# Gated cross-attention and feed-forward on one core: Q, K and V projected already turned, operands of the scores stacked by way of device memory

## The chip, the cores and the metric

The kernel runs on one core of a Trainium2 chip. The metric is the device time of one execution, in microseconds (us). The engines are TensorE (PE in the profile; its weight loads are PEld), VectorE (DVE), ScalarE (ACT), GpSimd (POOL) and SyncE (SP), which here only issues DMAs. A small q behind an engine's name, as in SPq, means its sequencer.

## What is computed

Eight batches of 128 tokens, 512 features each, go through a gated cross-attention and a gated feed-forward. There are 32 query heads of 16 features and 8 key/value heads, each shared by 4 query heads. All inputs are float32.

```python
x = x + tanh(g_xattn[0]) * xattn(layernorm(x), ctx, ctx, Wq, bq, Wk, bk, Wv, bv, Wo, bo)
x = x + tanh(g_ffn[0]) * ffn(layernorm(x), w1, w1_scale, w3, w3_scale, w2, w2_scale)

# xattn
Q = query @ Wq + bq; K = key @ Wk + bk; V = value @ Wv + bv    # heads: 8 x 4, 8, 8, of 16 features
scores = einsum('bhgqd,bhkd->bhgqk', Q, K) / sqrt(16)
w = softmax(scores, axis=-1)
y = einsum('bhgqk,bhkd->bhgqd', w, V)                          # back to 512 features
return y @ Wo + bo
# ffn, 512 -> 1792 -> 512, weights scaled by block of 128 x 128
h = silu(x @ w1.T) * (x @ w3.T); return h @ w2.T
```

## The kernel before

**Precision.** Every float32 operand of a matmul is split into a high part in TensorE's faster float32r form and the rest: names in H and L (`WpH` and `WpL`, `xTH` and `xTL`). A product is three matmuls, high by high, high by low, low by high; `three` at line 1765 issues them, which is why lines 1767 to 1769 carry most of TensorE's work. ACT makes most high parts and DVE or POOL most low ones.

**Attention, batch by batch.** POOL splits a tile of the context (`ct`) into `ctH` and `ctL`. DVE and POOL make the statistics of the layer norm, ACT writes the normalised `xn`, TensorE turns it (`turn4`) and ACT and DVE split the result into `xTH` and `xTL`. `project_kv` makes K and V (12 matmuls of 256 columns a batch) and `project` makes Q (12 of 512 columns); a further matmul each adds the bias (`add_bias`). In these the tokens are the stationary operand, so Q, K and V come out with tokens on the partitions. For the scores they are wanted with features on the partitions, and the three products of a score are folded into one matmul of 96 rows: 32 rows of high, 32 of low and 32 of high queries against high, high and low keys. So ACT and DVE write `Qtok` and `Ktok` with these copies side by side, TensorE turns them (`stack_q`, `stack_k`, through `identr`, line 1774; 24 turns a batch), and ACT copies the turned ones to `Qst` and to the stacked keys (`kst`, in the upper part of `x2HL`, which is not yet needed for its own purpose). V is cut into three bf16 parts in `Vp`.

**Scores.** `scores(n, h)` computes scores with queries on the partitions, only for their maximum along the keys (`row_max`, DVE, line 1142). The maxima are split in two (`Mtok`), turned to rows (`turn_max`), copied (`Mrow`) and moved by four small DMAs (`max_in`) into rows 96 to 99 of `Qst`, one pair of heads each; matching rows of the keys select the head. `scores_t(n, g)`, line 1819, computes the scores again with keys on the partitions and the maximum already subtracted. ACT takes its exponential twice, as float32 (`E`) and as f16 (`PH`), and POOL makes `PL`, the difference of the two (line 340, 64 of them). `values` multiplies with `Vp`; DVE sums the three parts and divides. The result is turned, projected with Wo in four blocks, added to `X`, normalised, turned and split into `x2H` and `x2L` (`x2HL`).

**Feed-forward.** 14 chunks of the 1792 features for two halves of four batches: `gu` computes both branches of a chunk, `y` the product back, 36 matmuls of 512 columns a chunk. POOL scales the weights (`scale`, line 351), ACT and DVE split them.

**Order.** All orders are written out by hand per engine: each engine's block issues its operations in one fixed sequence with semaphore waits between them. Queue SP loads in that order too, and a wait on SP holds back everything behind it. TensorE's list mixes projections of later batches, scores, values and the first chunks of the feed-forward. `W0`, `W1` and `W2` are three PSUM banks for whatever is turned or projected; two more hold the scores and two their transposed form, one the values.

## Time and profile before

| | us |
|---|---|
| median of 3 runs | 392.64 (391.22 to 392.65) |
| the profiled execution | 391.85 |
| its span, first to last instruction | 390.1 |
| TensorE busy | 377.4 |
| VectorE busy | 271.7 |
| ScalarE busy | 209.1 |
| GpSimd busy | 160.5 |

The profile is of one execution. Its span leaves out what lies around the program, 1.75 us here. Busy times are the time in which at least one instruction of an engine runs; matmuls overlap, so that two of 0.40 us may start 0.23 apart, and the sum of the durations is more than the busy time. An engine's idle time costs something only if another one waits for what it does later.

### The profile page before, as it was taken

The numbers are of one execution on the slowest core, as the hardware profiler recorded it, in microseconds if no ns is written. First come the engines' busy times: TensorE is split into PE (matmuls) and PEld (weight loads), VectorE is DVE, ScalarE is ACT, GpSimd is POOL, SyncE is SP. The second block draws the span as 40 slices with busy tenths as digits, with TensorE's granted clock in tenths as the row PEclk, the third lists the DMA queues.
The fourth block names the chain that finished last, engine by engine and source line by source line (L and its number), as shares of the span: only waits on it lengthen the run. The fifth ranks groups of instructions, "written<-read, shape, count | busy, mean of one in ns | idle before, by whom it ended". The sixth has DMA issues, their size and how long they took to land.

```text
span 390.1 us, 6293 instructions
## 1 busy us (share of the span) xinstructions
PE 377.4 (97%) x2350; PEld 307.5 (79%) x2350; DVE 271.7 (70%) x452; ACT 209.1 (54%) x367; POOL 160.5 (41%) x135
## 2 busy tenths in 40 slices
PE   7789999999998999999999999999999999999996
PEld 5578888888887677878888888888888888888885
DVE  5978998979998967898776777543954344554334
ACT  4678999998999986552332332332332332332320
POOL 6558889898999785264333443000000000000000
PEclk9999999999999999999999999999999999999999
DMA  8903104100000040295000000000200000000002
GB/s 289 342 14 86 32 2 167 46 40 6 2 6 3 3 166 2 86 416 227 0 0 0 0 0 0 0 0 2 108 0 0 0 0 0 0 0 0 0 0 108
DMA packets 6817, 20.98 MB, mean 54 GB/s; under 512 B 875, under 2 KB 1131, under 8 KB 6668
## 3 DMA queue, kind: packets, MB, share of 16 engines
q1 hardware_dynamic: 6364, 19.92, 14.0%
q10 hardware_dynamic: 432, 0.79, 0.5%
q8 instruction: 13, 0.21, 0.2%
q14 instruction: 8, 0.07, 0.0%
HBM read 18.28 MB, written 2.10 MB: 52 GB/s over the span
## 4 chain that ended last, share of the span: by engine, by line
PE 83%; DVE 9%; DMA 3%; SPq 2%; ACT 1%; issue 1%; POOL 0%; DVEq 0%
PE ps L1767 23%; PE ps L1769 23%; PE ps L1768 22%; PE ps L1819 3%; PE ps L1809 3%; PE ps L1774 3%; DMA gsc<-in_small 3%; DVE MX L1142 2%; PE ps L1827 2%; PE ps L1775 1%; PE ps L1828 1%; DVE x2HL L1172 1%; DVE X L1183 1%; DVE aTL L1153 1%; DMA Qst<-Mrow 1%
## 5 line engine op out<-in xcount | busy, mean ns | idle before, releaser
L1767 PE MATMUL ps<-x2HL,w13H 128*128 128x512 f32 x224 | 89.1, 398 | 0.0
L1769 PE MATMUL ps<-x2HL,w13L 128*128 128x512 f32 x224 | 88.6, 395 | 0.0
L1768 PE MATMUL ps<-x2HL,w13H 128*128 128x512 f32 x224 | 88.4, 395 | 0.0
L340 POOL TENSOR_TENSOR PL<-E,PH 128x512 f16<-128x512 f32 x64 | 74.1, 1174 | 13.2 <-ACT E L609 7.2
L351 POOL TENSOR_TENSOR wres<-wres,gsc 128x1536 f32<-128x1536 f32 x14 | 42.5, 3037 | 44.2 <-DVE hf L1196 44.2
L632 ACT ACTIVATE T<-ps 128x512 f32<-128x512 f32 x28 | 16.7, 597 | 79.0 <-PE ps L1769 79.0
L640 ACT ACTIVATE hH<-hf 128x512 fp32r<-128x512 f32 x28 | 17.7, 632 | 63.5 <-DVE hf L1196 63.5
L1769 PEld LDWEIGHTS ps<-x2HL,w13L 128*128 128x128 f32 x224 | 42.0, 187 | 10.4
L1768 PEld LDWEIGHTS ps<-x2HL,w13H 128*128 128x128 f32 x224 | 42.0, 188 | 9.8
L1189 DVE SCALAR_TENSOR_TENSOR A<-T,ps 128x512 f32<-128x512 f32 x28 | 19.2, 685 | 43.8 <-ACT T L632 43.8
L1767 PEld LDWEIGHTS ps<-x2HL,w13H 128*128 128x128 f32 x224 | 42.0, 188 | 9.5
L1767 PE MATMUL ps<-w2H,hH 128*128 128x512 f32 x112 | 44.3, 396 | 0.6 <-DVE x2HL L1172 0.6
L1205 DVE TENSOR_TENSOR hL<-hf,hH 128x512 fp32r<-128x512 f32 x28 | 43.2, 1541 | 2.5
L1769 PE MATMUL ps<-w2H,hL 128*128 128x512 f32 x112 | 43.8, 391 | 0.0
L1768 PE MATMUL ps<-w2L,hH 128*128 128x512 f32 x112 | 43.5, 389 | 0.0
L1142 DVE TENSOR_REDUCE MX<-ps 128x8 f32<-128x1024 f32 x32 | 38.9, 1215 | 4.6 <-PE ps L1809 4.6
L1196 DVE SCALAR_TENSOR_TENSOR hf<-A,ps 128x512 f32<-128x512 f32 x28 | 19.2, 687 | 32.5 <-PE ps L1769 32.2
L609 ACT ACTIVATE E<-ps 128x512 f32<-128x512 f32 x64 | 38.2, 612 | 1.8 <-PE ps L1819 1.6
L1177 DVE TENSOR_TENSOR w13L<-wres,w13H 128x1024 fp32r<-128x1024 f32 x28 | 34.1, 1219 | 5.1 <-ACT w13H L627 5.1
L612 ACT ACTIVATE PH<-ps 128x512 f16<-128x512 f32 x64 | 37.1, 606 | 1.0 <-PE ps L1819 0.6
L627 ACT ACTIVATE w13H<-wres 128x1024 fp32r (+1 forms) x28 | 29.3, 1045 | 0.0
L1819 PE MATMUL ps<-Qst,x2HL 100*128 100x512 f32 x64 | 27.3, 439 | 0.1
(112 smaller groups left out, 712.8 us busy)
## 6 DMA issues: line engine op xcount, KB each, us to landing
wres<-in_wff SPq DMA_DIRECT2D x14, 768.0 KB, 6.7
X<-in_x SPq DMA_DIRECT2D x8, 256.0 KB, 11.1
ct<-in_ctxt SPq DMA_DIRECT2D x7, 256.0 KB, 3.2
raw<-in_wproj SPq DMA_DIRECT2D x3, 512.0 KB, 6.3
out<-X SPq DMA_DIRECT2D x6, 256.0 KB, 2.0
raw<-in_wproj SPq DMA_DIRECT2D x1, 1024.0 KB, 9.4
Qst<-Mrow SPq DMA_DIRECT2D x32, 8.0 KB
out<-X ACTq DMA_DIRECT2D x2, 256.0 KB, 2.1
```

Of the source, the lines that this page charges most:

```text
L340: pool.tensor_tensor(PL[:, g % NL, :], E[:, g % NE, :], PH[:, g, :], ALU.subtract).then_inc(pL_ok, 1)
L351: pool.tensor_tensor(w, w, v, ALU.mult).then_inc(scaled, 1)
L609: act.activation(E[:, g % NE, :], ps[:, g % 2, :], ACT.Exp, scale=SCALE).then_inc(E_ok, 1)
L612: act.activation(PH[:, g, :], ps[:, g % 2, :], ACT.Exp, scale=SCALE).then_inc(PH_ok, 1)
L627: act.activation(w13H[:, s, :], wres[:, n, 0:W13], ACT.Copy).then_inc(w13H_ok, 1)
L1142: dve.tensor_reduce(MX[:, :, h, :], ps[:, 2:4, :].rearrange("p b (j g k) -> p (b j) g k", j=2, g=2), AX.X, ALU.max).then_inc(max_ok, 1)
L1177: dve.tensor_tensor(w13L[:, s, :], wres[:, n, 0:W13], r32(w13H[:, s, :]), ALU.subtract).then_inc(w13L_ok, 1)
L1205: dve.tensor_tensor(hL[:, s, :], hf[:, s, :], r32(hH[:, s, :]), ALU.subtract).then_inc(hL_ok, 1)
L1767: pe.matmul(out_ap, aH, bH, start=start, stop=False)
L1768: pe.matmul(out_ap, aH, bL, start=False, stop=False)
L1769: return pe.matmul(out_ap, aL, bH, start=False, stop=stop)
L1819: pe.matmul(ps[:, g % 2, :], kst(n)[0:ROWS + 4, g % 2, g // 2, :], Qst[0:ROWS + 4, n % 2, g // 2, :], start=True, stop=True).then_inc(st_p ...
```

## The change

Q, K and V are projected the other way round: the weights are the stationary operand and the tokens, of two batches at once, the moving one (256 columns). The features of Q, K and V then stand on the partitions without a turn, and the biases, now one number per partition, are added by ACT and DVE in the operation that copies the result out of PSUM (`q_high`, `k_high`, `v_bias`). V is turned back by two plain turns for each pair of batches (`turn_v`). To bring 32 rows of a pair of heads and the copies high, low, high above one another, the high and low parts go out to two tensors in device memory, `qscr` and `kscr`, and come back by one read of 32 rows for each of the three places (`queries_in`, `keys_in`; for the first batch by halves, `queries_part`).

The rows that carry the maxima are 16 and not 4, so `scores_t` contracts 112 rows and not 100, and one DMA brings them (`max_in`, 9 DMAs and not 32; the first batch has two). Scores are grouped by the query head in the group and not by the pair. Statistics have two slots each; some small operations went from DVE to POOL (`epsilon`, `shift`, `max_low`), and high parts of the context from POOL to ACT. The written orders of all five engines are new. Loads come in another order, and TensorE starts with 16 and not 14 warm-up matmuls.

```diff
+        qscr = nc.dram_tensor("qscr", [NBATCH // 2, 2, 2, P, GJ * P], F32).ap()
+        kscr = nc.dram_tensor("kscr", [NBATCH // 2, 2, P, 2, TWO], F32).ap()
...
+        def keys_out(eng, p, low):
+            eng.dma_start(kscr[p, low], r32((KTL if low else KTH)[:])).then_inc((kh_out, kl_out)[low], 16)
+
+        def keys_in(eng, p, t):
+            s = (NBATCH - NKST + 2 * p % NKST) * P
+            eng.dma_start(r32(kall(32 * t, 32 * t + 32)[:, :, s:s + TWO]),
+                         kscr[p, t % 2].rearrange("(r h) g n -> r (h g) n", h=PAIRS)).then_inc((k_in0, k_in1)[p % 2], 16)
...
+        def queries_in(eng, n, t, done):
+            eng.dma_start(r32(Qst[32 * t:32 * t + 32, n % 2, :, :]).rearrange("r h n -> r (h n)"),
+                         qscr[n // 2, t // 2, n % 2].rearrange("(r h) n -> r (h n)", h=PAIRS)).then_inc(done, 16)
...
+            sp.wait_ge(kT_H, 2)
+            keys_out(sp, 0, 0)
+            sp.wait_ge(kh_out, 16)
+            keys_in(sp, 0, 0)
+            sp.wait_ge(qT_H, 2)
+            queries_out(sp, 0, 0, 0, 2, qh_outa)
...
             sp.wait_ge(mrows, 5)
...
+            max_in(sp, 3, 0, 4)
+            sp.wait_ge(qh_out, 48)
+            sp.wait_ge(st_ps, 24)
+            queries_in(sp, 4, 0, q_in0)
+            queries_in(sp, 4, 1, q_in0)
...
+            def q_high(bank, j):
+                act.wait_ge(bias_in, 16)
+                act.activation(QTH[:, :, j, :], bank[:, 0:TWO].rearrange("p (b q) -> p b q", b=2), ACT.Identity,
+                               bias=biasT[:, BQ + j:BQ + j + 1]).then_inc(qT_H, 1)
...
+            def project_q(bank, j, k0, k1):
+                for k in range(k0, k1):
+                    c = Q0 + (j // 2) * KB * TWO + k * TWO + (j % 2) * P
+                    w = slice(c, c + P)
+                    m = three(bank[:, 0:TWO], WpH[:, w], WpL[:, w], xTH[:, k, :, :], xTL[:, k, :, :], k == 0, k == KB - 1)
+                return m
```

**Where instructions stand now.** TensorE at the start, before: the end of batch 0's Q projection, and all up to the first `scores` (line 1809).

```order
L1793 MATMUL ps<-brow,ones 128x512
L1774 MATMUL ps<-identr,Ktok 96x128 x4
L1775 MATMUL ps<-ident,xn 128x128 x4
L1774 MATMUL ps<-identr,Qtok 96x128 x8
L1774 MATMUL ps<-identr,Ktok 96x128 x4
L1774 MATMUL ps<-identr,Qtok 96x128 x4
L1809 MATMUL ps<-x2HL,Qst 128x256 x4
```

The same place after: the last rows before the first `scores` (line 1937), which are K and V of batches 2 and 3 and the turn of `xn` of batch 3.

```order
L1895 MATMUL ps<-ctH,WpH 128x256
L1896 MATMUL ps<-ctL,WpH 128x256
L1897 MATMUL ps<-ctH,WpL 128x256
L1903 MATMUL ps<-ident,xn 128x128 x4
L1937 MATMUL ps<-x2HL,Qst 128x256 x8
L1895 MATMUL ps<-xTH,WpH 128x256
```

The 20 turns through `identr` ahead of the first scores are gone; 96 matmuls of 256 columns stand there now, where there were 13 of 256 and 13 of 512.

SP after, at the start: from the first wait of its list on. `L209` loads Wo, `L206` tiles of X, `L212` `boT`; `L218` writes keys out and `L222` reads them, `L226` writes queries out and `L234` reads them.

```order
L245 DMA ct<-in_ctxt 128x512 [waits ctL_ok_dve]
L209 DMA raw<-in_wproj 128x2048
L206 DMA X<-in_x 128x512 x2
L212 DMA boT<-in_small 128x512
L218 DMA kscr<-KTH 128x512 [waits kT_H]
L222 DMA x2HL<-kscr 32x8x256 [waits kh_out]
L226 DMA qscr<-QTH 128x2x256 [waits qT_H]
L226 DMA qscr<-QTL 128x2x256 [waits qT_L]
L203 DMA x2HL<-sel 16x8x128
L222 DMA x2HL<-kscr 32x8x256 [waits kl_out]
L226 DMA qscr<-QTH 128x2x256 [waits qT_H,qT_H_dve]
L226 DMA qscr<-QTL 128x2x256 [waits qT_L]
```

Before, SP had nothing but loads there, the selection rows and, at its first wait for `mrows`, the rows of maxima.

SP after, in the middle: from the maxima of batch 3 to those of batch 4.

```order
L238 DMA Qst<-Mrow 16x4x512 [waits mrows]
L230 DMA Qst<-qscr 32x2048 [waits st_ps,qh_out]
L230 DMA Qst<-qscr 32x2048
L218 DMA kscr<-KTL 128x512
L230 DMA Qst<-qscr 32x2048 [waits st_ps]
L230 DMA Qst<-qscr 32x2048
L238 DMA Qst<-Mrow 16x4x512 [waits mrows]
```

Before, four DMAs of 4 rows stood behind each wait for `mrows` and nothing of the queries; now reads of the queries wait for the last `scores_t` of the batch whose place they take, with a third read of each batch in ACT's list.

## Rows read from the trace of the kernel before

**Rows 1.** Stretches: length, busy of PE, PEld, DVE, ACT, POOL; clock, DMA share, GB/s.

```profile
0.00:19.10 19.10, 13.77 (x68) 10.47 (x68) 14.04 (x28) 10.54 (x16) 11.14 (x25) 1.00 0.90 320
19.10:33.00 13.90, 12.62 (x102) 11.08 (x101) 10.46 (x20) 10.08 (x17) 8.72 (x6) 1.00 0.12 31
33.00:149.40 116.40, 114.25 (x1134) 95.26 (x1132) 103.18 (x235) 109.59 (x217) 102.50 (x90) 1.00 0.13 45
149.40:169.10 19.70, 19.33 (x120) 15.20 (x118) 16.16 (x33) 10.38 (x18) 8.26 (x7) 1.00 0.30 112
169.10:390.00 220.90, 217.48 (x936) 175.48 (x936) 127.87 (x139) 68.50 (x103) 29.86 (x10) 1.00 0.08 32
```

**Rows 2.** The longest wait of TensorE but the first: us in total, times, longest.

```profile
PE ps L1774 <- DVE Mtok L1149: 1.6, 3, 0.8
```

**Rows 3.** TensorE's groups by shape: count, then busy us and mean ns of one.

```profile
L1774 PE MATMUL ps<-identr,Qtok 128*96 128x128 f32 x128 | 13.7, 233 | 1.6 <-DVE Qtok L1127 1.2 <-ACT x2HL L615 0.3
...
L1774 PE MATMUL ps<-identr,Ktok 128*96 128x128 f32 x64 | 6.9, 231 | 0.3 <-DVE Ktok L1107 0.3
L1863 PE MATMUL ps<-Ktok 128*128 128x512 f32 x14 | 5.6, 578 | 1.8 <-DVE Ktok L1073 1.8
L1775 PE MATMUL ps<-ident,xn 128*128 128x128 f32 x32 | 5.0, 277 | 0.3 <-DVE vres L1118 0.2
```

**Rows 4.** TensorE's timeline from 20.31 us: start, duration, instruction.

```profile
20.31 0.28 PE L1769 MATMUL ps<-WpH,ctL 128*128 128x256 f32 x1
20.43 0.40 PE L1767 MATMUL ps<-WpH,xTH 128*128 128x512 f32 x1
20.66 0.39 PE L1768 MATMUL ps<-WpL,xTH 128*128 128x512 f32 x1
...
21.12 0.42 PE L1774 MATMUL ps<-identr,Qtok 128*96 128x128 f32 x4
21.37 0.70 PE L1809 MATMUL ps<-x2HL,Qst 96*128 96x256 f32 x4
```

**Rows 5.** ACT's groups by shape: the copies of turned queries and keys.

```profile
L619 ACT ACTIVATE Qst<-ps 96x512 fp32r<-96x512 f32 x32 | 18.7, 598 | 0.9 <-PE ps L1774 0.7
...
L615 ACT ACTIVATE x2HL<-ps 96x512 fp32r<-96x512 f32 x16 | 9.8, 612 | 2.0 <-PE ps L1774 2.0
```

**Rows 6.** DVE's groups by shape: the row maxima and their low parts.

```profile
L1142 DVE TENSOR_REDUCE MX<-ps 128x8 f32<-128x1024 f32 x32 | 38.9, 1215 | 4.6 <-PE ps L1809 4.6
...
L1149 DVE SCALAR_TENSOR_TENSOR Mtok<-MX,Mtok 128x32 fp32r<-128x32 f32 x8 | 2.4, 300 | 0.0
```

**Rows 7.** POOL's groups by shape between 33 and 152 us.

```profile
L340 POOL TENSOR_TENSOR PL<-E,PH 128x512 f16<-128x512 f32 x64 | 74.1, 1174 | 13.2 <-ACT E L609 7.2 <-ACT PH L612 5.4 <-PE ps L1828 0.2
L337 POOL TENSOR_TENSOR X<-X,boT 128x512 f32<-128x512 f32 x7 | 9.1, 1306 | 0.0
L351 POOL TENSOR_TENSOR wres<-wres,gsc 128x1536 f32<-128x1536 f32 x3 | 8.3, 2762 | 0.0
L334 POOL TENSOR_TENSOR ctL<-ct,ctH 128x512 fp32r<-128x512 f32 x5 | 6.4, 1288 | 0.0
L331 POOL TENSOR_TENSOR ctH<-ct,unit 128x512 fp32r<-128x512 f32 x4 | 4.2, 1038 | 0.6 <-DMA ct<-in_ctxt 0.6
L324 POOL TENSOR_TENSOR rs<-ve,neghalf 128x1 f32<-128x1 f32 x4 | 2.3, 566 | 0.7 <-DVE ve L1097 0.7
```

**Rows 8.** Timeline of the first 20 us: first statistics, first scores.

```profile
3.97 0.69 DVE L1091 BATCH_NORM_STATS2 st<-X 128x6 f32<-128x512 f32 x1
...
19.17 0.71 PE L1809 MATMUL ps<-x2HL,Qst 96*128 96x256 f32 x4
```

**Rows 9.** DMA: a store's issue to landing, maxima on the chain, a loading stretch.

```profile
out<-X SPq DMA_DIRECT2D x6, 256.0 KB, 2.0
...
58.82 2.29 DMA Qst<-Mrow
...
8.00:10.00 2.00, 1.04 (x7) 0.77 (x6) 1.32 (x2) 1.68 (x3) 0.00 (x0) 1.00 0.97 367
```

More of the change, by code:

```diff
@@ L1275, in _ @@
+            max_high(0, 2)
             dve.wait_ge(s_ps, 4)
[L1276 removed]
+            row_max(0, 3)
+            mean(5)
             dve.wait_ge(max_ok, 4)
[L1278 to L1289 removed]
@@ L1801, in stack_q, with project_kv @@
[L1801 to L1810 removed]
+            def project_kv(bank, w0, k0, k1):
+                for k in range(k0, k1):
+                    w = slice(w0 + k * KVD, w0 + (k + 1) * KVD)
+                    m = three(bank[:, 0:TWO], WpH[:, w], WpL[:, w], ctH[:, k, :, :], ctL[:, k, :, :], k == 0, k == KB - 1)
+                return m
```

2723 lines of the change are left out of this document (1338 added, 1385 removed).

## The prediction

> **What bounds the kernel now.** I read the stretches first: each engine's busy time in five pieces of the span, cut at the first `scores` (19.1 us), the first and the last `scores_t` (33.1 and 149.4) and the first matmul of `y` (169.1) [rows 1]. In the feed-forward stretch TensorE is busy 217.5 of 220.9 us and the others far less: only TensorE counts there. In the 116.4 us between the `scores_t` TensorE has 114.3, but ACT 109.6, DVE 103.2 and POOL 102.5: four engines with little room, and whatever relieves one meets the next. The waits of TensorE [rows 2] show how little is idle: the longest, apart from the one before the warm-up, is 1.6 us for DVE's `Mtok`, in three pieces. Only the first 33 us are another matter; there TensorE is busy 26.4 us, 5.6 of them warm-up matmuls [rows 3].
>
> TensorE's busy times overlap, so I price its work by the distance from one start to the next [rows 4]: a matmul of 256 columns takes 0.12 us (20.31 to 20.43), one of 512 takes 0.23 (20.43 to 20.66), four turns through `identr` 0.25 (21.12 to 21.37), so 0.063 each. The granted clock is 1.00, the 2.4 GHz level, in every stretch [rows 1].
>
> **The change, TensorE's work.** Gone are 128 turns of `Qtok` and 64 of `Ktok` [rows 3], 192 x 0.063 = 12.1 us, and 16 bias matmuls, eight of each width, 8 x 0.23 + 8 x 0.12 = 2.8. The Q projection goes from 96 matmuls of 512 columns to 192 of 256: 96 x 0.23 = 22.1 becomes 192 x 0.12 = 23.0, 0.9 more. K and V stay at 96 of 256. Eight plain turns of V come in, at no more than the 5.0 / 32 = 0.16 us of the turns of `xn` [rows 3]: 0.9 to 1.3. That is 14.9 - 0.9 - 1.1, some 13 us less; with the two new warm-up matmuls under the loads at nothing.
>
> **ACT, DVE, POOL.** ACT loses 32 copies to `Qst` at 0.60 and 16 to the stacked keys at 0.61 [rows 5], 29 us, and gets back some 25 half-width copies, at about 0.4: it drops out of the argument. DVE keeps its 32 reductions of 1.2 us [rows 6]; small operations on V and `Mtok` give way to half-width ones out of PSUM. I take 8 us less between the `scores_t`: 95. POOL keeps its 64 `PL` at 1.17 us, and loses less than TensorE does. Counted from its first `PL` to its last [rows 7]: 64 x 1.17 = 75.1; three `scale` at 2.76, 8.3; three bias additions instead of seven, 3.9; two `ctL` instead of four, 2.6; one `ctH`, 1.0; seven roots at 0.57, 4.0; seven `max_low` and eleven single-column operations that are new on POOL. No row has these on POOL. The nearest above is a root, 0.57, and below they cost at least nothing; I take 0.25, nearer to DVE's 0.30 for the same `Mtok` operation [rows 6], 4.5 in all. Sum 99.4 us (94.9 to 105.2), where before the same sum was 107.
>
> **The stretch between the `scores_t`, 116.3 us now.** By TensorE's order it loses 75 matmuls of 512 columns (177 to 102), gains 79 of 256 (169 to 248), and loses 144 small turns and 4 plain ones: -17.3 + 9.5 - 9.1 - 0.5 = -17.4, hence 98.9. That is more than a proportional share of the 13 us, since the projections of the first four batches' K and V now stand ahead of the first scores. But POOL wants 99.4 by then. Two engines cannot both be at 100% of a stretch while handing work to each other through four buffers of `E` and `PL`; before, the leader had 98% and the second 94%. I put POOL at 96%: 99.4 / 0.96 = **103 us**, a gain of 13 and not 17. The cover that hid POOL's sum was TensorE's own length, and it is gone.
>
> **The start, 33.1 us now.** Here the detour through device memory is bare. The high half of the keys is ready at about 14 us: X lands before 3.97 [rows 8], the first weights soon after, then come two normalisations, two turns and the projection. But its write stands in SP's ring behind what SP has asked for by 10 us: six tiles of X, three of `ct`, `boT`, Wv (11 x 0.25 MB), Wq and Wo (1 MB each), 4.75 MB, with 1.3 MB on ACT's ring drawing from the same engines. 6.1 MB (6.4 million bytes) at the 320 GB/s of the first 19 us [rows 1] is 20 us; the write itself 0.8 and the landing 1.5 more (a store lands 2.0 after its issue, issue 0.45 included [rows 9]): 22.3. SP waits there (`kh_out`), and so do all its later DMAs and, behind the same semaphore, ACT's `q_high(W2, 3)`, `normalise(2)` and its own reads. From 22.3 SP issues six DMAs at 0.55 and one selection read at 0.8 before the read of the queries, 26.4; it lands 2.3 us later, as a row of maxima does [rows 9], and a little more for its size: first `scores` at **29.3**, where now it is 19.17 [rows 8]. TensorE has done 13 us of projections by then and is idle some 8 us.
>
> Then DVE sets the pace: `row_max(0, 0)` is queued behind `x_low(3, W2)`, whose turn came just before the scores, to about 30.5. Four reductions at 1.2 make 35.4, split and subtraction 0.6 and 0.3 [rows 6] with waits 1.0, turn and copy 0.8, issue and landing 2.9 as for a row of maxima: first `scores_t` at **40**, 7 us later than now. From the first `scores` it has 11 us, as against 13.9 now, of which TensorE's own work is 9.
>
> **Edits with one answer.** In the feed-forward nothing but the place of two buffers changes: 220.9 stays. From the last `scores_t` to `y` there are 66 matmuls of 512 columns where 69 were, with four more plain turns: 19.7 becomes 19.4. The larger selection matrix costs POOL some 3 us before 7 us, under the loads. The maxima now go in one DMA of 16 rows and not in four of 4 rows at 0.58 us each of SP: no one waits longer.
>
> **The sum.** 40 + 103 + 19.4 + 220.9 = 383.3 us of span, where it is 390.1. The profiled execution took 391.85, 1.75 over its span; 385.1. The median of the runs is 0.8 above the profiled one, the lowest 0.6 below; I give 385.5.
>
> **Where a page speaks against it.** Six times, a stage's queries are read anew as soon as the last `scores_t` of the batch two before has let go of the `Qst` slot, and `scores` of the new batch stands 3.5 to 4.7 us of TensorE work behind it. Three reads of 256 KB each: issues to 1.1, landing 1.5, bytes 0.79 MB at the 367 GB/s of [rows 9] 2.1, so 4.7 after the slot is free; with waits elsewhere the stretch of TensorE is 4 to 5 long, a stall near nothing. That rate is one of tiles of 128 partitions; no row has a large read into 32. The Trainium skill, page "SBUF — State Buffer", section "Door 1: The DMA port swizzle", holds that partitions 0 to 31 reach only 8 of 16 ports, and measures 189 GB/s against 328 at 1 MiB. By that the three reads would move their bytes in 4.2 us and the stall would be about 2 us each time; the trace before can't tell, and I carry it as a rival.
>
> **The rivals.**
> A, the engines interlock better than I think: TensorE keeps the lead, the stretch is 98 us and the start 38 (the queue drains at the 367 GB/s of [rows 9], 2.5 us sooner). 38 + 98 + 19.4 + 220.9 + 2.2 = 378.5. For it: TensorE is busy 98% of the stretch with ACT at 94% and POOL at 88% beside it [rows 1]. Against: POOL's sum alone is 99.
> B, slower than before: reads into 32 rows move at half of 367 GB/s. Then each of six batches waits 6.8 - 4.4 = 2.4 us (14 us), and the first scores wait 1.5 more. 385.5 + 14 less what POOL catches up in those waits (its sum is then no bound, 4 us) = 395.5 to 397. It decides from about 1 us of stall a batch, where the gain is below measuring.
> C, the start is longer and nothing else: SP's blocking waits stack up (a read that lands 3 us late delays three more), TensorE comes back at the lower clock, where the warm-up matmuls took 0.40 each and not 0.23 [rows 3]. First `scores_t` at 45: 390.5, no change.
> D, the change doesn't do what it says, since the turns were hidden anyway: excluded for TensorE, busy 98% of the stretch [rows 1]; if POOL's unknown operations cost 0.57 each, the stretch is 105.2 / 0.96 = 109.6 and the time 392.
>
> **How the numbers follow.** Forecast 385.5 (382 to 389): 0.42. A: 0.26. B: 0.15. C: 0.10. D: 0.07. A measurement here tells some 0.5% from no change, 2 us: faster means under 390.7, slower over 394.6. Faster has the forecast, A and a little of C and D: 0.70. Slower has B and a tail: 0.16. Same 0.14. The range from 376 to 396 reaches from under A to the nearer part of B and leaves out some 2 in 10.
>
> **What would show it.** In the changed profile: no turns of `Qtok` and `Ktok`; the first `scores` near 29 us after an idle TensorE and the first `scores_t` near 40; the stretch between the `scores_t` at 103 with POOL busiest of all and waits of TensorE for `PL` and its releasers; the feed-forward unchanged at 221. Waits of the first `scores` matmul of a batch for a DMA of `Qst` above 1 us would mean B. The prediction is wrong if the first `scores` come before 25, or if the stretch is under 99 us or over 108.

## The result and the profile after

The changed kernel takes 417.11 us (median of 4 runs, 413.38 to 418.77), the kernel before 391.94 (4 runs, 391.22 to 392.65): ratio 1.063, 95% interval 1.054 to 1.072. The forecast was 385.5 us, the range ended at 396. The profiled execution took 418.76 us, one of the two longest of the four, so what is read from this one profile carries a spread of some 5 us.

The same five stretches as in [rows 1], cut at the same four matmuls (first `scores`, first and last `scores_t`, first matmul of `y`): length, busy of PE, PEld, DVE, ACT, POOL; granted clock, DMA share, GB/s.

```profile
span 417.0 us, 6079 instructions
0.00:32.20 32.20, 22.56 (x130) 19.90 (x130) 21.44 (x45) 17.31 (x28) 16.23 (x21) 0.93 0.87 283
32.20:46.60 14.40, 12.08 (x79) 11.90 (x80) 9.92 (x18) 4.24 (x9) 9.37 (x12) 0.79 0.89 212
46.60:174.00 127.40, 112.05 (x988) 92.46 (x986) 96.25 (x199) 87.08 (x168) 94.60 (x96) 0.87 0.48 127
174.00:194.40 20.40, 18.92 (x120) 14.98 (x119) 16.27 (x27) 7.16 (x13) 10.19 (x14) 1.00 0.41 159
194.40:417.00 222.60, 217.71 (x938) 175.32 (x936) 129.46 (x140) 69.99 (x104) 31.01 (x10) 1.00 0.07 27
```

| stretch, us | before | forecast | after |
|---|---|---|---|
| to the first `scores` | 19.1 | 29.3 | 32.2 |
| to the first `scores_t` | 13.9 | 10.7 | 14.4 |
| between the `scores_t` | 116.4 | 103 | 127.4 |
| to the first `y` | 19.7 | 19.4 | 20.4 |
| to the end | 220.9 | 220.9 | 222.6 |

Of the 33.7 us by which the span misses the forecast, 24.4 are in the middle, 6.6 at the start, 2.7 behind. And the clock is no longer at 2.4 GHz throughout: 0.93, 0.79 and 0.87 granted in the first three stretches, where [rows 1] had 1.00 everywhere. The page by 40 slices says where:

```profile
PE   6867979897897889997999999999999999999996
PEclk9896998896999759999999999999999999999999
DMA  8989682981544304019500000000020000000002
DMA packets 16949, 37.60 MB, mean 90 GB/s; under 512 B 1984, under 2 KB 7616, under 8 KB 16128
```

The clock dips again and again up to slice 15 of 40, that is through nearly all attention batches, and so does TensorE's busy share; the DMA engines move 37.6 MB (21.0 before), most of it by 160 us. What TensorE waits for in the whole span, beside [rows 2], where the longest wait was 1.6 us:

```profile
PE ps L1937 <- DMA Qst<-qscr: 15.6, 8, 2.5
PE ps L1903 <- DVE xTL L1221: 3.3, 1, 3.3
PE ps L1903 <- ACT xn L741: 2.2, 1, 2.2
PE ps L1895 <- DVE xTL L1221: 1.8, 2, 1.5
```

L1937 is `scores`: eight waits for the queries from device memory, six of them between the `scores_t`, one a batch from the third on. One of these in TensorE's timeline (start, duration, instruction, idle before):

```profile
110.02 0.18 PE L1957 MATMUL ps<-Vp,PL 128*128 128x49 bf16 x1
112.05 0.74 PE L1937 MATMUL ps<-x2HL,Qst 96*128 96x256 f32 x4 [1.85 <-DMA Qst<-qscr]
...
113.30 0.62 PE L1896 MATMUL ps<-WpL,aTH 128*128 128x512 f32 x1
113.72 0.63 PE L1897 MATMUL ps<-WpH,aTL 128*128 128x512 f32 x1
114.14 0.63 PE L1895 MATMUL ps<-WpH,aTH 128*128 128x512 f32 x1
114.57 0.63 PE L1896 MATMUL ps<-WpL,aTH 128*128 128x512 f32 x1
...
116.95 0.40 PE L1897 MATMUL ps<-WpH,aTL 128*128 128x512 f32 x1
```

TensorE is idle 1.85 us, and 1 us later its matmuls of 512 columns stand 0.43 us apart and last 0.63, where [rows 4] has 0.23 and 0.40: the 1.2 GHz level, for some 3.5 us. The wait is paid, and then the clock.

The issues of these reads (KB each, median us from issue to landing), at this wait and, below, between 31.3 and 42.4 us, where batch 1's are under way with much else:

```profile
Qst<-qscr SPq DMA_DIRECT2D x2, 256.0 KB, 4.7
Qst<-qscr ACTq DMA_DIRECT2D x1, 256.0 KB, 4.7
...
Qst<-qscr SPq DMA_DIRECT2D x2, 256.0 KB, 7.0
```

The first reads of a batch are asked for the moment its slot is free; from the first issue (106.36 us here) to the last landing (112.01) it is 5.65 us, over the six batches 5.6 to 6.9. The forecast had 4.7. The work that TensorE does between that first issue and its wait is 3.7 to 5.0 us in the six batches (3.8 here, to 110.20), about as forecast (3.5 to 4.7).

### The profile page after: what moved, and what is told of

Read it like the earlier page. It is cut to its first block, busy times and chain, and to the rows that moved or that the text cites. A ratio compares the mean times of both kernels' runs of the same rounds, so it can differ in the third digit from the quotient of the medians.

```text
span 417.0 us, 6079 instructions
## 1 busy us (share of the span) xinstructions
PE 383.3 (92%) x2248; PEld 314.6 (75%) x2248; DVE 273.3 (66%) x426; ACT 185.8 (45%) x318; POOL 161.4 (39%) x151
## 4 chain that ended last, share of the span: by engine, by line
PE 74%; DMA 14%; ACT 4%; DVE 4%; SPq 3%; issue 1%; ACTq 0%; DVEq 0%
PE ps L1895 21%; PE ps L1897 21%; PE ps L1896 20%; DMA Qst<-qscr 10%; PE ps L1937 4%; PE ps L1948 3%; PE ps L1903 2%; DMA ct<-in_ctxt 2%; ACT E L772 2%; ACT PH L775 1%; DMA kscr<-KTH 1%; DMA qscr<-QTH 1%; PE ps L1956 1%; PE ps L1957 1%; DVE MX L1261 1%
## 5 line engine op out<-in xcount | busy, mean ns | idle before, releaser
L455 POOL TENSOR_TENSOR PL<-E,PH 128x512 f16<-128x512 f32 x64 | 75.2, 1191 | 22.6 <-ACT E L772 9.4
L775 ACT ACTIVATE PH<-ps 128x512 f16<-128x512 f32 x64 | 38.3, 606 | 18.6 <-PE ps L1948 18.5
L1937 PE MATMUL ps<-x2HL,Qst 96*128 96x256 f32 x128 | 27.5, 351 | 17.4 <-DMA Qst<-qscr 15.6
L1937 PEld LDWEIGHTS ps<-x2HL,Qst 96*128 96x128 f32 x128 | 24.1, 249 | 21.9 <-issue 11.3
L1318 DVE TENSOR_TENSOR w13L<-wres,w13H 128x1024 fp32r<-128x1024 f32 x28 | 35.0, 1249 | 5.4 <-ACT w13H L790 5.4
```

What stands on the lines that cost most here:

```text
L455: pool.tensor_tensor(PL[:, g % NL, :], E[:, g % NE, :], PH[:, g, :], ALU.subtract).then_inc(pL_ok, 1)
L775: act.activation(PH[:, g, :], ps[:, g % 2, :], ACT.Exp, scale=SCALE).then_inc(PH_ok, 1)
L1318: dve.tensor_tensor(w13L[:, s, :], wres[:, n, 0:W13], r32(w13H[:, s, :]), ALU.subtract).then_inc(w13L_ok, 1)
L1937: m = pe.matmul(ps[:, b + h // 2, (h % 2) * TWO:(h % 2 + 1) * TWO], Qst[0:ROWS, n % 2, h, j * P:(j + 1) * P], kst(n)[0:ROWS, 2 * h:2 * h + ...
```

## The experiments

Sixteen more kernels ran, each beside the kernel before on the same chip (391.3 to 391.4 us). The time is the median of all executions of a kernel. "First `scores_t`" and "stretch" are of one profiled execution; the stretch is the one between the first and last `scores_t`. How far such a stretch can be trusted is seen on the kernels whose middle is that of the changed kernel, but for the split of Wo in some: e8, e3, e7, e14, the changed kernel itself and e10 have 122.7, 123.1, 124.5, 127.2, 127.4 and 127.9 us. A difference of under 5 us between two stretches shows nothing by itself. The profiles of e4, e8 and e16 are of their shortest executions (405.3, 417.2 and 400.9 us), that of e10 is of its longest (420.5).

| | time, us | ratio to before (95%) | first `scores_t` | stretch |
|---|---|---|---|---|
| after | 417.11 | 1.063 (1.054 to 1.072) | 46.6 | 127.4 |
| e1 reads left out | 398.32 | 1.017 (1.014 to 1.021) | 47.6 | 104.8 |
| e2 idle matmuls | 410.36 | 1.049 (1.045 to 1.053) | 46.8 | 118.6 |
| e3 reads in the quiet stretch | 414.68, once | | 46.8 | 123.1 |
| e4 reads into 96 rows | 407.27 | 1.039 (1.035 to 1.044) | 47.8 | 112.6 |
| e6 three places | 413.54 | 1.054 (1.046 to 1.062) | 45.5 | 116.2 |
| e7 turn first | 414.61 | 1.058 (1.055 to 1.061) | 46.6 | 124.5 |
| e8 Wo later | 422.40 | 1.083 (1.079 to 1.087) | 49.7 | 122.7 |
| e9 e6, e7 and e8 | 416.01 | 1.065 (1.060 to 1.070) | 49.0 | 115.8 |
| e10 start | 417.81 | 1.063 (1.057 to 1.069) | 47.7 | 127.9 |
| e11 maxima by ACT | 412.15 | 1.052 (1.049 to 1.055) | 48.0 | 119.3 |
| e12 e10 and e11 | 413.03 | 1.054 (1.051 to 1.058) | 46.8 | 120.8 |
| e13 maxima first | 407.85 | 1.042 (1.039 to 1.046) | 46.6 | 116.3 |
| e14 late loads | 418.37 | 1.064 (1.057 to 1.071) | 45.9 | 127.2 |
| e15 e13 and idle matmuls | 404.04 | 1.033 (1.028 to 1.039) | 46.0 | 113.5 |
| e16 e15, 64 rows | 403.89 | 1.032 (1.030 to 1.034) | 45.4 | 110.6 |
| e17 e16, reads first | 403.94 | 1.031 (1.028 to 1.035) | 44.9 | 113.6 |

### What the reads cost: e1

```diff
-            queries_in(sp, 2, 1, q_in0)
-            queries_in(sp, 2, 0, q_in0)
...
-            pe.wait_ge(q_in0, 96)
             scores(2, 0)
```

> Part left out: the reads of the stacked queries of batches 2 to 7 (18 reads of 256 KB) and TensorE's waits for them; the scores of these batches are made from what stands in the slot, everything else is as in the changed kernel. If the waits for these reads, with what the clock does after them, are the loss (theory R), the stretch between the first and the last scores_t falls from 127.4 us to 103 to 108 and the time from 417 to 393 to 398. If the new orders of the engines or POOL's sum are the loss (theory O), the stretch stays above 120 us and the time above 410. The start (first scores_t at 46.6) should not move under either.

398.32 us, and the stretch (same columns as above):

```profile
47.60:152.40 104.80, 98.92 (x987) 81.10 (x986) 95.37 (x199) 85.69 (x168) 94.28 (x95) 1.00 0.38 109
```

Theory R holds and O falls: by these two profiles 22.6 of the 24.4 us lost in the middle are the reads of the queries and what follows from waiting for them (18.3 if e3's 123.1 is taken for the changed kernel's stretch), and 1.8 are left for the new orders of the engines. The time falls by 18.8 us. The clock is 1.00 in this stretch. It also shows that reads at no cost would not have saved the change: 398.3 is 1.7% slower than before (1.4 to 2.1%), by the start, since the first `scores_t` is still at 47.6 us and not at 33.1.

### What the clock costs: e2

```diff
+                for _ in range(m):
+                    pe.matmul(bank, WpH[:, 0:P], WpH[:, 0:DM], start=True, stop=True)
...
+            fill(ps[:, 2, :], 9)
             pe.wait_ge(q_in0, 96)
             scores(2, 0)
```

> The changed kernel with nine matmuls of 512 columns on constant operands ahead of each of the six waits for the queries of batches 2 to 7, written to the bank that the scores overwrite next; 9 x 0.22 = 2.0 us, as long as the waits of 2.0 to 2.6 us. They do nothing useful, TensorE is only not idle. If a good part of the loss is the lower granted clock after each wait (theory C), scores start no later than now, the matmuls behind them go at 0.12 us a 256 columns and not 0.21, the granted clock of the stretch goes from 0.87 to 0.95 or more, and the stretch from 127.4 to about 116: time 404 to 408. If the clock costs nothing here, the time stays at 417, or grows by up to 3 us where the nine matmuls outlast the wait.

```profile
46.80:165.40 118.60, 112.22 (x1041) 91.97 (x1040) 95.10 (x199) 86.36 (x168) 94.64 (x96) 0.99 0.53 136
```

From TensorE's last useful matmul to the `scores` it is 12.2 us in the six places together, as long as before, but now filled with work that does nothing. The stretch is 8.8 us shorter by the two profiles (4.5 against e3's, which has the same waits, 12.0 us, and a clock of 0.90), the time 6.8 us, and the granted clock goes from 0.87 to 0.99. That is less than expected (404 to 408): theory C holds, its size was too high. With e1 the 22.6 us come apart: 12.2 are the six waits for `Qst<-qscr` in this stretch, 8.8 the clock behind them, 1.6 are left. The 1.6 may well be one wait that e2 has and the changed kernel has not, before a `scores_t`:

```profile
PE ps L1952 <- DMA Qst<-Mrow: 1.7, 1, 1.7
```

### Rows, bytes, latency: e3 and e4

e3 is the changed kernel with a series of reads in the quiet feed-forward stretch:

```diff
+                probe([(flat[0:32, :], src[0:32, :])])
+                probe([(E[:, 0, :], qscr[0, 0, 0])])
+                probe([(flat[32 * t:32 * t + 32, :], src[32 * t:32 * t + 32, :]) for t in range(3)])
+                probe([(E[:, t, :], qscr[0, t // 2, t % 2]) for t in range(3)])
+                probe([(flat[0:96, :], src[0:96, :])])
+                probe([(flat[0:64, :], src[0:64, :])])
+                probe([(flat[0:16, 0:512], src[0:16, 0:512])])
```

> The changed kernel with reads from device memory into a tile that is no longer used, issued by SP in the quiet feed-forward stretch, one after the landing of the one before, the series twice: one read of 256 KB into 32 rows, one of 256 KB into 128 rows, three into 32 rows each (rows 0, 32, 64), three into 128 rows each, one of 96 rows x 8 KB, one of 64 rows x 8 KB, one of 16 rows x 2 KB. If the few rows set the rate (theory P), one read into 32 rows takes over 0.6 us longer than one into 128, and three of them about 2 us longer than three into 128 rows, 5.5 against 3.7. If it is the way there and back (theory L), all series differ by their bytes at one rate, and even the small read takes over 2.5 us.

The DMA issues of the first series in the order of the list, one line for each entry (KB each, median us to landing):

```profile
E<-qscr SPq DMA_DIRECT2D x1, 256.0 KB, 3.3
...
E<-qscr SPq DMA_DIRECT2D x1, 256.0 KB, 2.7
...
E<-qscr SPq DMA_DIRECT2D x3, 256.0 KB, 4.2
...
E<-qscr SPq DMA_DIRECT2D x3, 256.0 KB, 3.1
...
E<-qscr SPq DMA_DIRECT2D x1, 768.0 KB, 5.3
...
E<-qscr SPq DMA_DIRECT2D x1, 512.0 KB, 4.7
...
E<-qscr SPq DMA_DIRECT2D x1, 32.0 KB, 1.7
```

From the first issue to the last landing, three reads into 32 rows took 5.5 us (5.4 in the second series), three into 128 rows 4.1 (4.5). The smallest took 1.7 (1.8). So both theories have a part, though theory L had put the small read above 2.5 us: some 1.7 us go by before even 32 KB have landed, and the bytes of three reads on top take 3.8 us into 32 rows and 2.4 to 2.7 into 128, 0.9 to 1.4 us less and not the 2 expected by P. 64 rows in one read (512 KB, 4.7 us) go no faster than two reads of 32 (the second landed 4.5 us after the first was asked for), and 96 rows in one (5.3, then 5.0) little faster than three times 32. The Trainium skill, page "SBUF — State Buffer", section "Door 1: The DMA port swizzle", holds that rows 0 to 63 reach no more ports than rows 0 to 31; the traces here agree with that, and with 32 rows being slower than 128, by a factor of 0.63 to 0.75 in the bytes' part (the page's 189 against 328 GB/s is 0.58).

e4 changes the shape in place:

```diff
+                c = slice(684 * t, min(684 * t + 684, PAIRS * GJ * P))
+                eng.dma_start(r32(Qst[0:ROWS, n % 2, :, :]).rearrange("r h n -> r (h n)")[:, c],
+                              qscr[n // 2].rearrange("l b (r h) n -> (l b r) (h n)", h=PAIRS)[0:ROWS, c]).then_inc(done, 16)
```

> Part changed: for batches 2 to 7 each of the three reads brings the same 256 KB into all 96 rows, a third of the columns each (96 rows x 2.7 KB and not 32 rows x 8 KB), from other places of the scratch, so the queries are not the right ones; numbers, bytes, queues and the waits for the slot are the same. Theory P (32 rows take the bytes at half the rate): the reads last 4.2 us or less and not 5.6 to 6.9, the waits of scores fall from 2.0 to 2.6 us to under 0.8, the stretch to 110 to 114, the time to 400 to 404. Theory L (latency and total bytes set the length): the waits stay above 1.6 us and the time above 412.

```profile
47.80:160.40 112.60, 101.13 (x987) 82.09 (x986) 95.24 (x199) 86.37 (x168) 94.43 (x95) 0.98 0.51 143
```

Its waits for the queries in this stretch:

```profile
PE ps L1948 <- DMA Qst<-qscr: 7.1, 6, 1.5
```

The time, 407.3, is between the two theories. (The queries that come in are not the right ones; their amount and the waits are.) The reads took 4.8 to 6.4 us, 0.1 to 1.3 less than in the changed kernel, and the six waits 7.1 us in all and not 12.2; the longest is 1.5. With waits 5.1 us shorter the stretch is 14.8 us shorter (the time 9.8), and behind the shorter waits the clock stayed up: 0.98 granted. The 5.1 and the 8.8 that e2 gives to the clock come to 13.9. That is the shape of this loss: over e1's stretch, 12.2 us of waits near 2 us each cost 22.6, and 7.1 us of waits near 1.2 each cost 7.8.

### Asking earlier: e6, e11, e13

```diff
+        def qst(n):
+            if n % 3 < 2:
+                return Qst[:, n % 3, :, :]
+            return Q3[:, :, :]
...
+            sp.wait_ge(qh_out, 32)
+            sp.wait_ge(ql_out, 32)
+            sp.wait_ge(woL_ok, 1)
+            queries_in(sp, 2, 0, q_in0)
+            queries_in(sp, 2, 1, q_in0)
+            queries_in(sp, 2, 2, q_in0)
             sp.wait_ge(mrows, 3)
             max_in(sp, 1, 0, 4)
```

> The changed kernel with three places for the stacked queries and not two: the third lies where the float32 Wo was, so the read of a batch can be asked for when scores_t of the batch three before is done, up to 18 us ahead of its scores; all three reads of a batch of 2 to 7 go on SP, still 32 rows each, the same bytes. The third chunk of feed-forward weights is loaded and scaled later for it. If the loss is that the read cannot start before the slot is free, whatever its rate (theory S), TensorE waits for none of batches 2 to 7, the stretch between the scores_t is 104 to 108 us as without reads, the time 397 to 401. If the bytes of the reads themselves are too many for the time they have, or disturb other work (theory P), waits above 1 us remain at three or more batches and the time is over 406.

413.54 us, above the 406 of theory P, but not for its reason: between the `scores_t` TensorE waits for no queries. What is there in their place (waits in this stretch and, last, one behind it):

```profile
PE ps L1958 <- issue: 3.0, 1, 3.0
...
PE ps L1958 <- DMA Qst<-Mrow: 1.9, 2, 1.7
PE ps L1958 <- DMA Q<-Mrow: 1.5, 1, 1.5
...
PE ps L1913 <- ACT x2n L763: 3.8, 1, 3.8
```

L1958 is `scores_t`, which needs the rows of maxima; the 3.0 us put down to "issue" stand before the first `scores_t` of batch 1, whose maxima landed then. I had put the reads ahead of the maxima on SP. The 3.8 us are another slip of the edit: POOL's moved `scale(2)` holds ACT, and so `x2n`. e11 lets ACT ask for the maxima and moves that `scale`:

```diff
-            sp.wait_ge(mrows, 3)
-            max_in(sp, 1, 0, 4)
...
             max_rows(W0, 0, 4)
+            act.wait_ge(mrows, 3)
+            max_in(act, 1, 0, 4)
```

> The kernel with three places for the queries, and two edits on what it showed: the rows of maxima of batches 1 to 7 are asked for by ACT, behind its own copy, and not by SP, where they stood in the ring behind the reads of the next batch's queries (TensorE waited 1.6 to 3.1 us for them three times); and the third feed-forward chunk is scaled by POOL a batch earlier, since its old new place cost one wait of 4.0 us. Theory Q (what took the place of the wait for queries is the ring in front of the maxima): the waits for Mrow fall under 0.7 us, the stretch from 116.2 to 106 to 109, the time from 413.5 to 400 to 403. If the transfers as such are too many at that time, the waits stay over 1.5 us in any order and the time is above 408.

412.15 us: the maxima were later still. Their DMA on ACT's queue for batch 2, issued at 73.0 us, and below it the same one in the changed kernel on SP's, issued at 73.9 (us to landing):

```profile
Q<-Mrow ACTq DMA_DIRECT2D x1, 128.0 KB, 8.6
```

```profile
Qst<-Mrow SPq DMA_DIRECT2D x1, 128.0 KB, 3.6
```

Nothing stood ahead of it in ACT's queue. But SP asked for 2.5 MB between 71.8 and 75.8 us (queries out, keys in, a weight chunk), 1.5 MB of it before this DMA, since no wait for the maxima held it back any more. The two queues share the DMA engines; the Trainium skill, page "DMA: Bandwidth & Descriptors", says so under "Issuing engines are not separate DMA queues", and the trace agrees, 8.6 us against 3.6. In the changed kernel SP's wait for `mrows` is what keeps the bulk behind the maxima: the same transfers are asked for there from 74.6 us on. e13 makes use of that: three places, SP, and the maxima ahead of the reads.

```diff
-            queries_in(sp, 2, 0, q_in0)
-            queries_in(sp, 2, 1, q_in0)
-            queries_in(sp, 2, 2, q_in0)
             sp.wait_ge(mrows, 3)
             max_in(sp, 1, 0, 4)
+            queries_in(sp, 2, 0, q_in0)
+            queries_in(sp, 2, 1, q_in0)
+            queries_in(sp, 2, 2, q_in0)
```

> Three places for the queries, with the maxima of batches 1, 3 and 5 asked for by SP ahead of the reads of the next batch and ahead of the waits for the scratch, and the third feed-forward chunk scaled a batch earlier. Theory T (the DMA engines serve what was asked for first, on whichever ring: the maxima asked for by ACT landed 8.6 us later behind 2.5 MB that SP had asked for, and 3.1 us later with nothing ahead): all maxima land in under 4.5 us, TensorE waits for neither queries nor maxima more than 1 us between the scores_t, the stretch is 105 to 109 us, the time 398 to 402. If the waits for the maxima had another cause, they stay at 1.5 to 4 us and the time is above 408.

407.85 us, under e11 by 4.3. All maxima now land within 4.1 us of their issue, as theory T expects, but T's time (398 to 402) is missed: the waits went back to the queries (stretch between the `scores_t`):

```profile
PE ps L1947 <- DMA Qst<-qscr: 5.1, 2, 3.4
...
PE ps L1947 <- DMA Q<-qscr: 1.0, 1, 1.0
```

They are before batches 2, 4 and 6, the first of each pair, whose queries must first be written to device memory. So of 127.4 - 104.8 = 22.6 us a third place brings back 11; the other half I did not get by order. The order of the transfers moved waits more than it removed them: e6 has the same stretch, 116.2 us, with 6.4 us of waits for maxima where e13 has 6.1 for queries. The 5.7 us between the times of e6 and e13 lie behind the stretch, where e6 had the slip with `x2n` (26.1 us to the first `y`, 20.6 in e13).

### The start: e7, e8, e9, e10, e12, e14

```diff
-            pe.wait_ge(q_in1, 48)
-            scores(1, 0)
             pe.wait_ge(mL_ok, 2)
             pe.wait_ge(qT_L, 5)
             turn_max(W0, 2, 4)
+            pe.wait_ge(q_in1, 48)
+            scores(1, 0)
```

> The changed kernel, one piece of TensorE's list in another order: the turn of batch 0's last two maxima ahead of scores(1, 0), which waits for batch 1's queries (landed at 42.2 us), and not behind it. If that wait is what holds the first scores_t (it blocks the turn, 2.4 us in the profile), the first scores_t comes at 43 to 44.5 us and not at 46.6, and the time falls by 2 to 3 us to 414 or 415. If DVE's maxima set it as forecast (the last of batch 0 ends at 39.7 us), the turn gains nothing and the time stays at 417.

The first `scores_t` stayed at 46.6. The profile of e7 does not show the wait at all: TensorE was at the lower level there, had no pause from 37 to 42 us, and came to `scores(1, 0)` just after its queries had landed (42.2).

```profile
37.00:42.00 5.00, 5.00 (x26) 4.94 (x26) 3.12 (x6) 1.37 (x3) 1.22 (x4) 0.50 0.93 238
...
42.34 0.71 PE L1937 MATMUL ps<-x2HL,Qst 96*128 96x256 f32 x4
...
46.60 0.39 PE L1948 MATMUL ps<-Qst,x2HL 112*128 112x512 f32 x1
```

In the changed kernel these two matmuls are at 42.33 and 46.59. `scores(1, 0)` stands ahead of `scores_t(0, 0)` in both lists, with 4.3 us of matmuls from the one to the other at the full clock; what is moved ahead of the wait cannot shorten that. The time, 414.6, has an interval that overlaps that of the changed kernel.

```diff
-            out_weights_in(sp)
...
             queries_part(sp, 0, 1, 2, 4, q_in0)
+            out_weights_in(sp)
```

> The changed kernel, with the 1 MB load of Wo behind the reads of batch 0's queries on SP and not ahead of the first write of keys; ACT and POOL split Wo some 20 us later. If the write of the keys waits in the ring behind these bytes (issued at 15.7, landed at 21.3 us), it lands by 18.5 us, the first scores come at 29 to 30 and not at 32.3, the first scores_t at 43.5 to 44.5, the time falls by 2 to 3 us. If the lists of ACT and DVE set the start, the keys land earlier but the first scores stay above 31.3 us and the time within 1 us of 417.

The first write of keys, issued at 15.7 and 15.5 us, in the changed kernel and in e8:

```profile
kscr<-KTH SPq DMA_DIRECT2D x1, 256.0 KB, 5.6
```

```profile
kscr<-KTH SPq DMA_DIRECT2D x1, 256.0 KB, 3.2
```

As expected it lands 2.4 us earlier, and so come the first `scores`, at 29.8 us (forecast 29.3). But the first `scores_t` is 3 us later, and the time 5 longer: the 1 MB of Wo now stands ahead of batch 1's queries, which land at 43.4 us and not 42.2, and the second half of batch 0's queries lands late as well (35.5). e9 has this, the turn and the three places in one:

> The three edits together: a third place for the queries, the turn ahead of the waiting scores, Wo behind the queries' reads. By theory S, and if the two edits of the start each give 2 to 3 us, 399 - 5 = 392 to 396 us, that is still no faster than the kernel before at 391.4; TensorE's work is some 12 us less and the start eats 9 of it. If the start's two edits meet the same limit, only one of them counts and the time is 396 to 398.

416.01 us, 2.5 more than e6 alone, whose slip it carries too: the start's loss (first `scores_t` at 49.0) outweighs. e10 puts batch 1's reads ahead of Wo and of three other tiles:

```diff
-            context_in(sp, 5)
-            select_rows(sp, 3)
             queries_in(sp, 1, 0, q_in1)
+            queries_in(sp, 1, 1, q_in1)
+            out_weights_in(sp)
+            select_rows(sp, 3)
```

> The changed kernel with four moves at the start: Wo out of the way of the first write of keys, as before, but behind the reads of batch 1's queries; those reads ahead of three tiles of ct and X in SP's list; and batch 0's turn of maxima ahead of scores(1, 0). Theory W (the reads of batch 1, landed at 42.2 us behind 1.8 MB of other transfers in SP's ring, hold TensorE at scores(1, 0), and with it scores_t(0, 0), which stands behind): they land by 37 us, the first scores_t comes at 42 to 43.5 and the time is 412 to 414. If ACT's and DVE's lists set the start, the first scores_t stays above 45.5 us and the time above 415.5.

These queries landed at 37.4 us and not 42.2, and the first `scores_t` was still at 47.7; the second half of batch 0's queries came later instead (36.3), and TensorE ran at the lower level:

```profile
30.00:37.00 7.00, 3.73 (x17) 3.47 (x18) 2.68 (x3) 0.30 (x1) 3.04 (x3) 0.50 1.02 271
37.00:42.00 5.00, 5.00 (x26) 4.94 (x26) 3.12 (x6) 0.99 (x2) 0.97 (x4) 0.50 0.87 267
```

This profile is of e10's longest execution (420.5 us), but the other three took 414.2 to 418.8, none in the 412 to 414 of theory W, and e12, which has the same start, shows the same in a usual one: queries landed at 36.8 us, granted clock 0.52 from 30 to 37 us and 0.65 from 37 to 42, first `scores_t` at 46.8. Theory W falls in this form. e12 adds e11 to it, and they don't add up:

> The edits of the start and those of the middle in one kernel. If they add up, first scores_t at 42 to 43.5, stretch 106 to 109, time 396 to 400: still slower than the kernel before (391.4) by what the start costs. If the start's gain is lost in the middle (SP's list is one), the time is 400 to 403 as without it.

413.03 us, against 412.15 for e11 alone. e14 leaves less to be moved before the first `scores_t`, with Wo and a tile of `ct` behind batch 0's maxima.

```diff
             max_in(sp, 0, 2, 4)
             keys_in(sp, 1, 0)
+            context_in(sp, 6)
+            out_weights_in(sp)
```

> The changed kernel with less asked for ahead of batch 0's maxima: Wo and a tile of ct (1.25 MB) behind them, batch 1's queries ahead of the other tiles, and the turn of maxima ahead of scores(1, 0). Wo is split 10 us later on ACT and POOL. Theory T applied to the start (bytes asked for ahead of what is waited for set it: with Wo between the reads of batches 0 and 1 the first scores came 2.5 us earlier and the first scores_t no earlier): first scores at 29.8, batch 1's queries landed by 35 us, first scores_t at 41.5 to 43.5, and the time 412 to 414 if the later split of Wo costs nothing. If ACT's and DVE's lists are the limit of the start, the first scores_t is at 46 or later although the transfers land earlier.

First `scores` at 29.4, batch 1's queries landed at 36.6, first `scores_t` at 45.9; TensorE has a wait of 2.5 us for `E` and one of 1.8 for `PL` that the changed kernel has not, which I put down to the late split of Wo, and the time is 418.4. The clock between 32 and 42 us was 0.50 to 0.56 here too: from 37 to 42 us TensorE worked without a pause while the DMA engines were busy a quarter of the time.

### The clock at the start, and a wider read: e15, e16, e17

```diff
+            fill(14)
             pe.wait_ge(xn_ok, 4)
...
+            fill(5)
             pe.wait_ge(k_in0, 48)
...
+            fill(9)
             pe.wait_ge(q_in1, 48)
```

> The kernel of e13 (three places, maxima ahead of the reads) with matmuls of 512 columns on constants in TensorE's remaining waits: five more warm-ups, 14, 5 and 9 ahead of the last turn of xn, the first scores and scores(1, 0), and 5, 8 and 14 ahead of the waits for the queries of batches 2, 4 and 6. They do nothing useful. Theory C (the clock after a wait costs about as much as the wait): the granted clock is 0.99 or more from the first scores on, the first scores_t comes 2 to 3 us earlier (43.5 to 44.5), the stretch falls from 116.2 to 108 to 111, the time from 407.9 to 398 to 402. If only the waits themselves cost, the time stays within 1.5 us of 407.9.

Five more warm-ups, and 5, 8 and 14 such matmuls ahead of the queries of batches 2, 4 and 6, go with it. 404.04 us, 3.8 less than e13, where 6 to 10 were expected. Its clock is 1.00 up to the first `scores_t`, and yet the first `scores_t` is at 46.0:

```profile
32.00:37.00 5.00, 4.72 (x40) 4.45 (x39) 4.69 (x6) 0.99 (x2) 3.46 (x4) 1.00 1.01 217
37.00:42.00 5.00, 2.87 (x15) 2.12 (x15) 0.77 (x4) 0.37 (x1) 3.44 (x5) 1.00 1.00 245
```

With the faster clock TensorE has its work done sooner and waits to 41.7 us for batch 1's queries. So theory C is wrong for the start: two limits lay side by side there, and mending one showed the other. In the middle it has the sign right and the size too high: the stretch falls from 116.3 to 113.5 (108 to 111 expected) at a clock of 0.98 instead of 0.94. e16 sends the high and low copies to 64 rows at once:

```diff
+                eng.dma_start(r32(qst(n)[0:64, :, :]).rearrange("r h n -> r (h n)")[:, c],
+                             qscr[n // 2, n % 2].rearrange("l (r h) n -> (l r) (h n)", h=PAIRS)[:, c]).then_inc(done, 16)
```

> e15 with the first two of the three reads of batches 2 to 7 going to 64 rows (high and low copies, half of the columns each, 64 rows x 4 KB) and not to 32 rows x 8 KB; the same bytes, the right queries, the scratch laid out by batch for it. If few rows cost time in the place where the reads are still late, the reads of batch 6 land 0.5 to 1 us earlier and the time is 1 to 2 us under e15. If not, since the series in the quiet stretch took 512 KB into 64 rows in 4.6 us, no faster per byte than 32 rows, the time equals that of e15 within 0.5%.

403.89 against 404.04 us: no difference, as e3's 64 rows had led to expect (the shorter stretch in the table, 110.6, is of an execution 3 us under that median). e17 is to mend both limits of the start at once: reads first as in e10 (Wo where it was), and the idle matmuls of e15 but for the nine ahead of `scores(1, 0)`.

> e16 with batch 1's queries asked for ahead of two tiles of ct and one of X, the turn of maxima ahead of scores(1, 0), and no idle matmuls ahead of scores(1, 0); Wo stays where it was. At the full clock of e15 and e16 TensorE still waited there to 41.7 and 41.1 us for these queries; where the same order was tried alone, they landed at 37.4, but TensorE was at the lower clock. If the two together set the start, scores(1, 0) starts by 39 us, the first scores_t at 42.5 to 44 (45.4 in e16), and the time is 400.5 to 402.5 (403.9 in e16). If the start is now set by ACT's and DVE's lists, the first scores_t stays above 45 and the time at 404.

`scores(1, 0)` starts at 37.9 and not 41.1 us, but the first `scores_t` only at 44.9 and not 45.4, and the time is the same, 403.94. What ends TensorE's waits in between are now `QTL` and `Mrow`:

```profile
37.67 0.28 PE L1917 MATMUL ps<-identr,Mtok 128*16 128x128 f32 x2 [0.45 <-DVE QTL L1247]
39.69 0.39 PE L1910 MATMUL ps<-xTH,WpH 128*128 128x256 f32 x1 [1.02 <-ACT Mrow L809]
```

The second wait has its root in ACT's list, where the write of the keys of batches 2 and 3 must have landed before ACT copies the maxima to `Mrow`. And it costs more than its 1.02 us. Behind it TensorE works without a pause to the first `scores_t`, but at the lower level up to 43.4 us (matmuls of 256 columns 0.21 us apart and not 0.12); the stretch from the turn to that `scores_t` has a granted clock of 0.76:

```profile
39.27 0.37 ACT L809 ACTIVATE Mrow<-ps 16x256 fp32r<-16x256 f32 x1 [3.07 <-DMA kscr<-KTH]
...
40.22 0.41 PE L1910 MATMUL ps<-xTH,WpH 128*128 128x256 f32 x1
40.44 0.41 PE L1911 MATMUL ps<-xTL,WpH 128*128 128x256 f32 x1
...
37.67:44.86 7.19, 6.16 (x37) 5.80 (x37) 3.99 (x7) 2.74 (x6) 5.03 (x7) 0.76 0.74 225
```

So e17 did not have both limits mended: the clock fell again. From `scores(1, 0)` to the first `scores_t` it takes 6.9 us, where e15 and e16 need 4.3 at the full clock. Next in line are the rows of maxima, which landed at 44.2 us, 0.6 before the first `scores_t` (46.0 and 46.6 in the changed kernel). Whether the start would be shorter with that copy ahead of ACT's wait, no run shows.

No version I found is faster than the kernel before; the best, at 403.9 to 404.0, are 3.1 to 3.3% slower.

## Why the prediction was wrong

**The work of the engines: right.** TensorE's work in the middle was put at 98.9 us; e1, without the reads and at the full clock, has it busy for 98.92. DVE was put at 95 us, it has 95.1 to 96.3. The saving was there: e1's stretch is 11.6 us shorter than before.

**POOL as the bound: the sum was right, its use was not, and 103 came near 104.8 by luck.** From the first `PL` to the last, as the forecast counted, POOL's operations add up to 100.5 us in e1 (99.4 forecast); the unknown `max_low` at 0.25 took 0.254 (x7), the single-column operations 0.23 to 0.26. But the first and last `PL` stand 106.5 us apart there, beyond the ends of the stretch, in which POOL is busy only 94.3 us of 104.8, 90%, and TensorE 98.9, 94%. TensorE keeps the lead, and the 0.96 by which I divided has no support in these runs.

**The step that failed: the stall "near nothing".** Its parts were: issues to 1.1, landing 1.5, bytes 2.1 at 367 GB/s, 4.7 us in all, against TensorE work of 4 to 5. The work was right: 3.7 to 5.0 us. The reads were not: measured from the same first issue they take 5.6 to 6.9. e3's series, with the DMA engines otherwise idle, takes 5.5, some 1.7 of it before the smallest read has landed and 3.8 for the bytes into 32 rows (207 GB/s and not 367). The other 0.1 to 1.4 us I put down to other traffic, which the forecast left out of the sum; no run separates that part. I took the rate of [rows 9] for a shape that has no row, at the very place where the margin was nothing, and gave the rival that has it right 0.15.

**Rival B had the mechanism.** It asked for waits above 1 us before the first `scores` of a batch, six of 2.4 us, 14 us. There are six, of 12.2 us together. The time it gave, 395.5 to 397, was still 20 us too low: no case had a price for the clock in the middle (8.8 by e2's profile), B took 4 us off for a bound by POOL that was none, and its start was 5 us too early. Rival C knew of the lower level, but only at the start, where its 45 us for the first `scores_t` came nearer than my 40. The row to reason from was there: [rows 3] has the warm-up matmuls at 0.58 us each where TensorE had been idle before (the column of the clock says 1.00 even there, so the durations must be read), and [rows 1] and [rows 2] show a kernel at 1.00 throughout in which the longest wait of TensorE but the first comes to 1.6 us, in pieces of at most 0.8. A change that puts six waits of about 2 us into such a kernel must be priced with part of the work behind each wait at half speed; here that is some 7 us for 12.2 us of waits (e2: 6.8 of the time, 4.5 to 8.8 of the stretch).

**The start: 46.6 us, forecast 40.** The first `scores` came at 32.2 and not 29.3. The queue model was near: the first write landed at 21.3 (22.3 forecast), and with Wo out of its way at 18.7 (e8), and the first reads of batch 0's queries went out at 26.8 (26.4). What failed is again the length of these reads: the third could be asked for only at 28.4, when the write of the low part had landed, and it landed at 32.1, 5.3 us after the first issue where I had 2.9. From the first `scores` I gave 10.7 us to the first `scores_t`, with DVE's maxima in the lead and TensorE's own work at 9. It took 14.4. The work is about 9.6 at the full clock (e16: busy 11.8 with nine idle matmuls in it). The step missing is that `scores(1, 0)`, with reads that landed only at 42.2 us, stands in TensorE's list ahead of `scores_t(0, 0)`, with 4.3 us of work between them; and the clock, 0.79 in this stretch.

**Behind it.** 20.4 and 222.6 us for 19.4 and 220.9: the second carries a wait of 1.6 us for `hL` at the first `y`, which the changed kernels have and the kernel before has not. I had called the stretch unchanged without reading DVE's new list at its head.

**Sum.** By the profiles: reads and clock in the middle 22.6, start 6.6, behind 2.7, the stretch itself 1.8: 33.7 us on a span of 383.3.

## What to carry to other kernels

Moving a reshuffle from a compute engine to device memory changes work that can be queued into a wait whose length is set by the transfer's own time in its own shape and by what else is in the DMA engines: before doing it, compare the time from the release of the buffer to the last landing, other traffic included, with the work that stands behind that release, and where the margin is under a microsecond or two, count on the wait. On a kernel that TensorE bounds at the full clock, price a wait of 2 us with the slower work behind it, here 1.4 to 1.7 times its length in all (12.2 us of waits and 4.5 to 8.8 behind them). A small transfer on the critical path must be asked for before the bulk, on whichever queue, and a wait that looks like it only holds a queue back may be what keeps that order.

## What was not expected of the hardware

The granted clock made the loss uneven: six waits that were shorter by 0.9 us each (e4) shortened the stretch by 14.8 us and the time by 9.8. In e17 even a wait of 1.02 us was followed by some 3.5 us at the lower level. A 128 KB transfer alone in ACT's queue landed 8.6 us after its issue behind 1.5 MB asked for by SP, with 1 MB more asked for right behind it, and 3.2 to 3.6 us without them. And at the start two limits hid each other: earlier transfers alone (e10, e14), and the full clock alone (e15), each left the first `scores_t` where it was to within 1.1 us.
